# Graph-attention block on one core: value parts side by side in the attention product, head halves added on GpSimd

## The chip, the cores and the metric

The kernel runs on one core of one Trainium2 chip. The metric is device time in microseconds (us) of one execution, the median of several executions of the same program. Lower is better.

## What is computed

The reference chains two layers over 384 nodes with 1,024 features: a dense graph attention with 16 heads of width 64 (with a mask made of 6,144 edges), a linear attention and a quantised feed-forward block, then a second layer with a graph convolution of four hops, another linear attention and a mixture of eight experts. The change touches the 16-head attention, in float32 throughout:

```python
q2, k2, v2 = (each (N, H*D)).reshape(N, H, D).transpose(1, 0, 2)      # N = 384, H = 16, D = 64
scores = einsum('hnd,hmd->hnm', q2, k2) * 0.125 + mask[None]
attn = softmax(scores, axis=-1)
out = einsum('hnm,hmd->hnd', attn, v2).transpose(1, 0, 2).reshape(N, 1024)
return out @ wo.T + bo
```

## The kernel before, in words

Every engine has its own instruction stream, and all streams walk the same list of steps (`STEPS`, built by `schedule()`), each taking from a step what is its part. Nothing is reordered at run time: an engine that waits holds everything behind it in its stream.

Products in float32 precision are made of three passes of a faster format (fp32r): an operand is split into a high part (ScalarE: `hi_part`, a rounding copy) and a low part (VectorE: `lo_part`, the difference), and TensorE adds high x high, high x low and low x high. Weights come in 140 units of 128x1024: SyncE loads `raw`, ScalarE makes `w_hi` (L955), VectorE makes `w_lo` (L1263), three units ahead of TensorE (`AHEAD`), in a ring of four (`RING`).

The attention stage lies from about 218 to 357 us. For a head h the steps are `scores` (TensorE, L2014: two matmuls for each of three tiles of 128 rows; VectorE, L1580: moves each tile out of its bank, adds the mask and takes the row maximum; then L1585 makes `nmax` from the three maxima), `exps` (ScalarE, L1099), `normalise` (VectorE, L1596 and L1598), `probs` (TensorE transposes, L1829; ScalarE and VectorE make the two parts of `probT`) and `attend`: the product of probabilities and values. Two heads later the next scores are under way, and units of the next projections fill TensorE between: `k2` and `q2` up to head 11, the first five units of the output projection `wo` from head 12 on. A `k2` unit ends in `kcat` (ScalarE L946, VectorE L1472, and GpSimd copies it by two DMAs), a `q2` unit in `qcat`. Both use bank 0, so that a `q2` unit starts when VectorE has emptied the `k2` unit before it. `scores` reuses its banks when VectorE has moved the scores of the head before out of them.

In `attend` of head h the values are loaded as 128 columns, those of the even and of the odd head of a pair, so each product yields 128 rows, of which 64 are the head's own. High and low part of v2 are separate planes, and it takes nine matmuls. ScalarE and VectorE split the head's 64 rows into `oT`.

After the last head come `ffn_mean`, then the rest of `wo`: unit 5 ends the first half of the columns (c = 0), units 6 to 11 are the second half (c = 1), the last four of them row tile by row tile (L2069). ScalarE has between them `w_open` and `w_cast`, two long casts of feed-forward weights. VectorE moves the first half out by `wo_out(0, t)` (L1348, statistics behind it, L1278 and L1355), for three tiles, between the splits of later units; the feed-forward block starts on VectorE with `wo_out(1, 0)` in the step `in_stats`, when tile 0 of the second half is complete.

`wo_out` adds the product to `base1`, an array in SBUF that holds x and two bias rows. GpSimd makes it: SyncE loads x, then GpSimd issues three accumulating DMAs of the row `bo`, waits for them to land, and issues three of the row `mix_bo` (L812). Its code stands at the step of the last head:

```python
if s[0] == "attend" and s[1] == H0 - 1:
    pool.wait_ge(x_landed, 16)
    for t in range(NT):
        add_row("bo", t, base1).then_inc(bo_added, 16)
    pool.wait_ge(bo_added, 16 * NT)
    for t in range(NT):
        add_row("mix_bo", t, base1).then_inc(base1_ready, 16)
```

and the first line of `wo_out` is `dve.wait_ge(base1_ready, 16 * NT)`. Before the change GpSimd has no part in any other `attend` step; in that stage its stream holds only the copies of `kcat` and table work for the graph.

Of the kernel before, what the change touches and what calls it, by code (L numbers as in the profile page):

```python
# [5 lines left out]
F32 = mybir.dt.float32  # L6
# [9 lines left out]
P = 128  # L16
# [64 lines left out]
def schedule():  # L81
# [76 lines left out]
    run("wo", 5, 6)  # L158
    steps.append(("w_open",))
    run("wo", 6, 7)  # L160
# [132 lines left out]
def plan_banks():  # L293
# [12 lines left out]
    for s in STEPS:  # L306
        kind = s[0]
        if kind == "unit":
            _, u, name, i = s
            if name in FEATURE_MAJOR:  # L310
                if name in ("v1", "mk"):
                    product(f"{name}.{i}", i % 3 + 3 * (name == "mk"), u)
                elif name in ("q2", "k2"):
                    product(f"{name}.{i}", {("k2", 0): 1, ("k2", 1): 1, ("q2", 0): 4, ("q2", 2): 1}.get((name, i), 0), u)
                else:
                    product(f"{name}.{i}", i % 6 if name == "e1" else single % 6, u)
                    single += 1
            else:
                per = NODE_MAJOR[name][1]
                if i % per == 0:  # L320
                    for t in range(NT):

                        b = {("wo", 0): (0, 6, 1), ("e2", 0): (4, 5, 0), ("e2", 8): (1, 2, 3)}.get((name, i), tuple(range(
                            3 * (group % 2), 3 * (group % 2) + 3)))[t]
                        product(f"{name}.{i // per}.{t}", b, UNIT_OF[(name, i + per - 1)] if t == NT - 1 else None)
                    group += 1
# [86 lines left out]
def gps_kernel(nc, weights, x_in, edges, rows, cols, tiny, w1_in, w2_in, gate_in, eb2_in, out):  # L413
    with ExitStack() as ctx:
# [48 lines left out]
        v2 = at("v2", [P, 2, NT, D], F32R, R2)  # L463
# [4 lines left out]
        prob = at("prob", [P, 2, NT, N], F32, AT + 12)  # L468
        probT = at("probT", [P, 2, NT, N], F32R, AT + 21)
# [141 lines left out]
        s_max, s_exp, p_ready = sem("s_max"), sem("s_exp"), sem("p_ready")  # L611
# [14 lines left out]
        h_scaled = sem("h_scaled")  # L626
        out_ready, out_stored = sem("out_ready"), sem("out_stored")
# [52 lines left out]
        def row(name, a=0, b=None):  # L680
            return row_sb[:, row_slot(name)[0], a:sum(q - p for _, p, q in LOADS[name][1]) if b is None else b]

# [92 lines left out]
        def _(pool):  # L775
# [65 lines left out]
            for s in STEPS:  # L841
# [54 lines left out]
                if s[0] == "degree":  # L896
                    wait_emptied(pool, "degree")
                    pool.tensor_tensor(dis[:, 1], dis[:, 0], minus_half[:, 0:NT], ALU.pow).then_inc(dis_ready, 1)
                if s[0] == "attend" and s[1] == H0 - 1:

                    pool.wait_ge(x_landed, 16)
# [37 lines left out]
        def _(act):  # L939
# [58 lines left out]
            for s in EVAC_STEPS:  # L998
# [24 lines left out]
                if kind == "unit":  # L1023
# [23 lines left out]
                    if name in NODE_MAJOR and i % NODE_MAJOR[name][1] == NODE_MAJOR[name][1] - 1:  # L1047
                        c = i // NODE_MAJOR[name][1]
                        for t in range(NT):
                            pr = f"{name}.{c}.{t}"  # L1050
                            sl = slice(c * HALF, (c + 1) * HALF)
                            if name == "v2":
                                wait_emptied(act, pr)
                                hi_part(v2[:, 0, t, sl], v2f[:, t, sl])
# [39 lines left out]
                if kind == "exps":  # L1094
                    h = s[1]
                    act.wait_ge(s_max, h + 1)
                    for t in range(NT):

                        act.activation(prob[:, h % 2, t], prob[:, h % 2, t], ACT.Exp, scale=0.125,  # L1099
# [9 lines left out]
                if kind == "attend":  # L1109
# [4 lines left out]
                    hi_part(TT["o"][hs, 0, h // 2], out_of(f"attend.{h}")[hs, 0:N], f"attend.{h}")  # L1114
# [118 lines left out]
        def _(dve):  # L1233
# [170 lines left out]
            for s in EVAC_STEPS:  # L1404
# [50 lines left out]
                if kind == "unit":  # L1455
# [33 lines left out]
                    if name in NODE_MAJOR and i % NODE_MAJOR[name][1] == NODE_MAJOR[name][1] - 1:  # L1489
                        c = i // NODE_MAJOR[name][1]  # L1490
                        sl = slice(c * HALF, (c + 1) * HALF)
                        if name in ("v2", "v"):
# [7 lines left out]
                            for t in range(NT):  # L1500
                                wait_emptied(dve, f"{name}.{c}.{t}")
                                if name == "v2":
                                    low, high, src = v2[:, 1, t, sl], v2[:, 0, t, sl], v2f[:, t, sl]
# [63 lines left out]
                if kind == "scores":  # L1567
# [5 lines left out]
                    if h >= 1:  # L1573
                        dve.wait_ge(s_max, h)
# [25 lines left out]
                if kind == "attend":  # L1600
                    h = s[1]
                    hs = slice(64 * (h % 2), 64 * (h % 2) + 64)
                    lo_part(TT["o"][hs, 1, h // 2], out_of(f"attend.{h}")[hs, 0:N], TT["o"][hs, 0, h // 2], f"attend.{h}")
# [205 lines left out]
        def _(pe):  # L1809
# [35 lines left out]
            for s in STEPS:  # L1845
# [31 lines left out]
                if kind in ("unit", "part", "first_k"):  # L1877
# [44 lines left out]
                    else:  # L1922
# [7 lines left out]
                        for kk in [n % per for n in here]:  # L1930
# [6 lines left out]
                            elif name == "wo":  # L1937
# [3 lines left out]
                                if c == 0 and kk >= 2:  # L1941
                                    wait_emptied(pe, f"attend.{4 * kk - 5 - 2 * (kk == per - 1)}")
# [74 lines left out]
                if kind == "probs":  # L2017
                    h = s[1]
                    pe.wait_ge(p_ready, NT * (h + 1))
                    for m in range(NT):  # L2020
                        transposes(f"pT.{h}.{m}", [prob[:, h % 2, t, m * P:(m + 1) * P] for t in range(NT)])
                if kind == "attend":
# [5 lines left out]
                    js = slice(h // 2 * P, (h // 2 + 1) * P)  # L2028
# [57 lines left out]
                if kind == "in_T":  # L2086
                    t = s[1]
                    pr = f"xqT.{t}"
                    pe.wait_ge(in_quant, t + 1)
                    wait_bank(pe, pr)  # L2090
# [167 lines left out]
```

## Time and profile before

| | us |
|---|---|
| median of three runs | 756.64 |
| lowest and highest | 756.59, 757.14 |
| span of the profiled execution | 755.6 |
| TensorE busy in the span | 733.0 |
| VectorE busy | 547.4 |
| ScalarE busy | 391.2 |
| GpSimd busy | 193.3 |

The span runs from the first to the last instruction of the profiled execution, whose own total time is not listed apart; the median of the runs is 1.0 us above the span. The span is therefore used for differences, and the median for the total. A busy TensorE means that matmuls follow one another without a gap. A 384-column matmul shows about 334 ns from start to end, but a new one starts about every 174 ns, so counts are multiplied by the distance of starts.

### The profile page before, as it was taken

The page shows a single profiled execution, that of the slowest core. Times are in us where ns is not written, and L with a number is a line of the kernel's source. Part 1 is how long each engine was busy: PE and PEld are TensorE (multiplying, and loading weights), DVE is VectorE, ACT ScalarE, POOL GpSimd, SP SyncE. Part 2 cuts the span into 40 slices and gives each one's busy share as a digit, 9 for nine tenths or more (in the row PEclk, how much of TensorE's full clock was granted, in tenths as well). Part 3 has the DMA queues.
Part 4 walks back from the last instruction along what each step waited for, and adds up shares of the span by engine and source line. Part 5 has one row for each costly group of instructions (what it writes and reads, how often), then busy time and mean ns, then how long its engine had stood idle before and what let it go on. Part 6 is the DMA issues. An engine that isn't in the chain of part 4 may idle for free. (4 is left out here: it accounts for less than half of the span.)

```text
span 755.6 us, 10696 instructions
## 1 busy us (share of the span) xinstructions
PE 733.0 (97%) x3884; PEld 655.2 (87%) x3884; DVE 547.4 (72%) x1071; ACT 391.2 (52%) x802; POOL 193.3 (26%) x194
## 2 busy tenths in 40 slices
PE   5999999999999999999988999999999989999998
PEld 4999888999999999988755888888888889998886
DVE  6898885654569999876878687899966776674331
ACT  5533334644748767666665464854753342553220
POOL 5358888864205520021032110000020020000000
PEclk9999999999999999999999999999999999999999
DMA  7876555436434442499453582332352363244331
GB/s 253 304 208 170 115 137 140 112 85 224 142 105 130 101 109 77 164 286 267 136 137 112 152 227 88 134 122 74 112 125 84 119 131 137 96 142 151 126 126 42
DMA packets 38532, 107.71 MB, mean 143 GB/s; under 512 B 12424, under 2 KB 12600, under 8 KB 38096
## 3 DMA queue, kind: packets, MB, share of 16 engines
q1 hardware_dynamic: 25360, 89.90, 35.4%
q0 software_dynamic: 12912, 15.00, 12.5%
q10 hardware_dynamic: 208, 2.12, 0.8%
q8 instruction: 31, 0.51, 0.3%
q14 instruction: 21, 0.17, 0.1%
HBM read 96.31 MB, written 2.83 MB: 131 GB/s over the span
## 5 line engine op out<-in xcount | busy, mean ns | idle before, releaser
L1263 DVE TENSOR_TENSOR w_lo<-raw,w_hi 128x1024 fp32r<-128x1024 f32 x140 | 170.0, 1222 | 71.1 <-ACT w_hi L955 70.7
L955 ACT ACTIVATE w_hi<-raw 128x1024 fp32r<-128x1024 f32 x140 | 147.5, 1057 | 102.3 <-PE bank L1970 81.1
L1918 PE MATMUL bank<-xn1T,w_hi 128*128 128x384 f32 x416 | 106.1, 335 | 0.0
L1970 PE MATMUL bank<-w_hi,xn3T 128*128 128x512 f32 x288 | 92.6, 394 | 0.0
L816 POOL DMA_INDIRECT count_table<-total,place x48 | 82.9, 1727 | 26.5 <-issue 14.3
L1918 PEld LDWEIGHTS bank<-xn1T,w_hi 128*128 128x128 f32 x416 | 74.9, 188 | 0.1
L1918 PE MATMUL bank<-xn1T,w_lo 128*128 128x384 f32 x208 | 69.5, 334 | 0.0
L1970 PEld LDWEIGHTS bank<-w_hi,xn3T 128*128 128x128 f32 x288 | 54.1, 188 | 11.0
L816 POOL DMA_INDIRECT mask_table<-value,place x48 | 54.1, 1126 | 31.0 <-issue 13.1
L1918 PE MATMUL bank<-xn4T,w_hi 128*128 128x384 f32 x240 | 61.1, 335 | 0.0
L1970 PE MATMUL bank<-w_lo,xn3T 128*128 128x512 f32 x144 | 56.0, 389 | 0.0
L1918 PEld LDWEIGHTS bank<-xn4T,w_hi 128*128 128x128 f32 x240 | 43.2, 188 | 0.0
L1918 PE MATMUL bank<-xn4T,w_lo 128*128 128x384 f32 x120 | 40.2, 335 | 0.0
L1918 PEld LDWEIGHTS bank<-xn1T,w_lo 128*128 128x128 f32 x208 | 39.0, 188 | 0.0
L1099 ACT ACTIVATE prob<-prob,nmax 128x384 f32<-128x384 f32 x48 | 29.1, 609 | 10.9 <-DVE nmax L1585 10.7
L922 POOL DMA_DIRECT2D x_sb<-g x3 | 2.6, 1200 | 120.1 <-DVE g L1718 120.1
L890 POOL DMA_DIRECT2D kcat<-kcat x16 | 8.7, 546 | 96.1 <-DVE kcat L1472 95.2
L1918 PE MATMUL bank<-q1T,w_hi 128*128 128x384 f32 x128 | 33.1, 339 | 0.1
L1918 PE MATMUL bank<-k1T,w_hi 128*128 128x384 f32 x128 | 32.5, 335 | 0.0
L1970 PEld LDWEIGHTS bank<-w_lo,xn3T 128*128 128x128 f32 x144 | 27.1, 188 | 5.3
L1970 PE MATMUL bank<-w_hi,yT 128*128 128x512 f32 x96 | 31.0, 394 | 0.0
L1970 PE MATMUL bank<-w_hi,hT_a 128*128 128x512 f32 x96 | 30.6, 389 | 0.0
(353 smaller groups left out, 1682.7 us busy)
## 6 DMA issues: line engine op xcount, KB each, us to landing
raw<-weights SPq DMA_DIRECT2D x140, 512.0 KB, 3.6
row_sb<-rows SPq DMA_DIRECT2D x6, 512.0 KB, 6.0
kcat<-kcat POOLq DMA_DIRECT2D x16, 192.0 KB, 2.9
base<-rows POOLq DMA_DIRECT2D x6, 512.0 KB, 13.0
w1r<-w_in ACTq DMA_DIRECT2D x1, 2048.0 KB, 8.8
w2r<-w_in SPq DMA_DIRECT2D x1, 2048.0 KB, 10.3
x_sb<-x_in SPq DMA_DIRECT2D x3, 512.0 KB, 5.0
row_sb<-rows SPq DMA_DIRECT2D x6, 256.0 KB, 5.1
```

Of the source, the lines that this page charges most:

```text
L816: return pool.indirect_dma_start(tab[:, :], bass.IndirectOffsetOnAxis(ap=place[:, n:n + 1].bitcast(U32), axis=0), src, None, **how)
L890: pool.dma_start(f(kcat[other, r]), f(kcat[own, r])).then_inc(k_twice, 16)
L922: pool.dma_start(x_sb[:, t, HID:D], g[:, t], accum_op=ALU.add).then_inc(base3_ready, 16)
L955: act.activation(w_hi[:, u % RING], raw[:, u % RAW], ACT.Copy).then_inc(hi_split, 1)
L1099: act.activation(prob[:, h % 2, t], prob[:, h % 2, t], ACT.Exp, scale=0.125, bias=nmax[:, h % 2, t:t + 1], accum_out=rsum[:, h % 2, t:t + ...
L1263: dve.tensor_tensor(w_lo[:, u % RING], raw[:, u % RAW], f(w_hi[:, u % RING]), ALU.subtract).then_inc(unit_split, 1)
L1918: last = pe.matmul(out_of(pr)[:, 0:N], w[pa][:, slot, k * P:(k + 1) * P], TT[src][:, pb, k], start=(k == 0 and m == 0), stop=(k == KD - 1 ...
L1970: last = pe.matmul(out_of(pr)[:], tile[:, pa, k, ts], w[pb][:, at_, j * HALF:(j + 1) * HALF], start=(kk == 0 and j == 0 and m == 0 and nam ...
```

## The change

The parts of v2 lie side by side for each head: 64 columns of the high part, 64 of the low part. One matmul with the high part of `probT` then gives high x high in output rows 0 to 63 and the correction in rows 64 to 127, and `attend` has six matmuls in place of nine (with the low part of `probT`, the rows 64 to 127 get low x low too). The two halves must be added: ScalarE copies the lower 64 rows into `o_rest`, and after each odd head GpSimd adds `o_rest` (128x384, both heads of the pair) to the low part of `oT`. TensorE waits for that addition (`o_low`) where it reads `oT`, and for ScalarE's copy (`rest_kept`) before the bank is written again. The eviction of scores takes a scale of -0.125 and a minimum, so that it yields `nmax` and L1585 goes; ScalarE's exponentials wait for one tile at a time. In `wo`, unit 6 goes ahead of unit 5, with banks (4, 5, 3).

```diff
-    run("wo", 5, 6)
+    unit("wo", 6)
+    unit("wo", 5)
     steps.append(("w_open",))
-    run("wo", 6, 7)
     steps.append(("w_cast", 1))
...
-        v2 = at("v2", [P, 2, NT, D], F32R, R2)
+        v2 = at("v2", [P, NT, H0, 2 * DH], F32R, R2)
...
+        def v2_part(part, t, sl):
+            return v2[:, t, sl.start // DH:sl.stop // DH, part * DH:(part + 1) * DH]
...
         # GpSimd, ahead of the block for the step attend, H0 - 1
+                if s[0] == "attend" and s[1] % 2:
+                    j = s[1] // 2
+                    wait_emptied(pool, f"attend.{s[1]}")
+                    pool.wait_ge(rest_kept, s[1] + 1)
+                    pool.tensor_tensor(TT["o"][:, 1, j], f(TT["o"][:, 1, j]), o_rest[j % 2][:], ALU.add).then_inc(o_low, 1)
                 if s[0] == "attend" and s[1] == H0 - 1:
...
         # ScalarE
-                    act.wait_ge(s_max, h + 1)
+                        wait_emptied(act, f"scores.{h}.{t}")
-                        act.activation(prob[:, h % 2, t], prob[:, h % 2, t], ACT.Exp, scale=0.125,
+                        act.activation(prob[:, h % 2, t], prob[:, h % 2, t], ACT.Exp, scale=-1.0,
...
-                    hi_part(TT["o"][hs, 0, h // 2], out_of(f"attend.{h}")[hs, 0:N], f"attend.{h}")
+                    hi_part(TT["o"][hs, 0, h // 2], out_of(f"attend.{h}")[0:DH, 0:N], f"attend.{h}")
+                    if h >= 4:
+                        act.wait_ge(o_low, h // 2 - 1)
+                    act.activation(o_rest[h // 2 % 2][hs], out_of(f"attend.{h}")[DH:2 * DH, 0:N], ACT.Copy).then_inc(rest_kept, 1)
...
         # VectorE
-                        emptied(dve.tensor_tensor_reduce(out=prob[:, b, t], in0=out_of(pr)[:, 0:N], in1=mask[:, t], scale=1.0,
-                                                         scalar=-3.0e38, op0=ALU.add, op1=ALU.max,
-                                                         accum_out=top1[:, 0, t:t + 1]), pr)
-                    for t in range(NT):
-                        wait_emptied(dve, f"scores.{h}.{t}")
-                    dve.tensor_scalar(nmax[:, b], top1[:, 0], -0.125, None, ALU.mult).then_inc(s_max, 1)
+                        emptied(dve.tensor_tensor_reduce(out=prob[:, b, t], in0=out_of(pr)[:, 0:N], in1=mask[:, t], scale=-0.125,
+                                                         scalar=3.0e38, op0=ALU.add, op1=ALU.min,
+                                                         accum_out=nmax[:, b, t:t + 1]), pr)
...
         # TensorE
-                                    wait_emptied(pe, f"attend.{4 * kk - 5 - 2 * (kk == per - 1)}")
+                                    pe.wait_ge(o_low, 2 * kk - 2 - (kk == per - 1))
...
-                                wait_emptied(pe, f"attend.{H0 - 1}")
+                                pe.wait_ge(o_low, H0 // 2)
...
+                    if h:
+                        pe.wait_ge(rest_kept, h)
                     for m in range(NT):
                         pe.wait_ge(act_hi, hi_at[f"pT.{h}.{m}"])
-                        for part in (HI, LO):
-                            pe.matmul(out_of(pr)[:, 0:N], v2[:, part, m, js], probT[:, HI, m], start=(m == 0 and part == HI), stop=False)
+                        pe.matmul(out_of(pr)[:, 0:N], v2[:, m, h], probT[:, HI, m], start=(m == 0), stop=False)
                     for m in range(NT):
                         wait_emptied(pe, f"pT.{h}.{m}")
-                        last = pe.matmul(out_of(pr)[:, 0:N], v2[:, HI, m, js], probT[:, LO, m], start=False, stop=(m == NT - 1))
+                        last = pe.matmul(out_of(pr)[:, 0:N], v2[:, m, h], probT[:, LO, m], start=False, stop=(m == NT - 1))
```

## Rows read from the trace of the kernel before

**Rows 1.** The page, busy time of each engine

```profile
PE 733.0 (97%) x3884; PEld 655.2 (87%) x3884; DVE 547.4 (72%) x1071; ACT 391.2 (52%) x802; POOL 193.3 (26%) x194
```

**Rows 2.** Timeline of weight loads (PEld): start, length, engine, line, count, idle before

```profile
301.20 0.30 PEld L2014 LDWEIGHTS bank<-kcat,qcat 128*128 128x128 f32 x2 [0.18 <-DVE top L1580]
...
305.68 1.05 PEld L2033 LDWEIGHTS bank<-probT,v 128*128 128x128 f32 x6
306.72 0.53 PEld L2036 LDWEIGHTS bank<-probT,v 128*128 128x128 f32 x3
307.24 1.08 PEld L1829 LDWEIGHTS bank<-ident,prob 128*128 128x128 f32 x9
...
317.17 0.30 PEld L2014 LDWEIGHTS bank<-kcat,qcat 128*128 128x128 f32 x2 [0.18 <-DVE top L1580]
```

**Rows 3.** Timeline of VectorE over one pair of heads

```profile
290.75 1.26 DVE L1472 SCALAR_TENSOR_TENSOR kcat<-bank,bias,kcat 64x384 fp32r<-64x384 f32 x2 [0.86 <-ACT kcat L946]
...
293.48 0.09 DVE L1580 DVE_READ_ACCUMULATOR2_ANT top<- 128x1 f32 x1
293.70 0.17 DVE L1585 TENSOR_SCALAR nmax<-top 128x3 f32<-128x3 f32 x1
293.90 0.56 DVE L1254 TENSOR_TENSOR oT<-bank,oT 64x384 fp32r<-64x384 f32 x1
...
306.72 0.61 DVE L1472 SCALAR_TENSOR_TENSOR kcat<-bank,bias,kcat 64x384 fp32r<-64x384 f32 x1 [0.87 <-ACT kcat L946]
```

**Rows 4.** Groups of ScalarE in the attention stage, 215 to 375 us

```profile
L946 ACT ACTIVATE oT<-bank 64x384 fp32r<-64x384 f32 x16 | 7.8, 485 | 20.7 <-PE bank L2036 20.7
```

**Rows 5.** Busy time by stretch: TensorE, loads, VectorE, ScalarE, GpSimd, clock, DMA

```profile
350.00:355.00 5.00, 5.00 (x29) 4.30 (x28) 3.17 (x5) 4.57 (x6) 0.00 (x0) 1.00 1.06 236
360.00:365.00 5.00, 5.00 (x24) 4.14 (x23) 4.96 (x5) 4.81 (x3) 0.00 (x0) 1.00 0.04 13
```

**Rows 6.** Timeline of all engines after the last head's product

```profile
357.12 0.49 ACT L946 ACTIVATE oT<-bank 64x384 fp32r<-64x384 f32 x1 [0.51 <-PE bank L2036]
...
357.64 0.56 DVE L1254 TENSOR_TENSOR oT<-bank,oT 64x384 fp32r<-64x384 f32 x1 [3.37 <-ACT oT L946]
...
363.22 1.22 DVE L1263 TENSOR_TENSOR w_lo<-raw,w_hi 128x1024 fp32r<-128x1024 f32 x1
...
364.36 0.69 DVE L1348 CUSTOM_DVE_ANT_0 base<-bank,base 128x512 f32<-128x512 f32 x1
...
370.12 3.48 DVE L1263 TENSOR_TENSOR w_lo<-raw,w_hi 128x1024 fp32r<-128x1024 f32 x3
...
371.39 0.19 PEld L2069 LDWEIGHTS bank<-w_hi,oT 128*128 128x128 f32 x1 [0.88 <-DVE w_lo L1263]
...
375.92 0.69 DVE L1348 CUSTOM_DVE_ANT_0 base<-bank,base 128x512 f32<-128x512 f32 x1 [2.31 <-PE bank L2069]
```

**Rows 7.** Timeline of GpSimd, 320 to 380 us

```profile
326.36 2.73 POOL L812 DMA_DIRECT2D base<-rows  x3 [1.04 <-issue]
344.19 2.60 POOL L812 DMA_DIRECT2D base<-rows  x3 [15.09 <-DMA base<-rows]
377.69 0.19 POOL L868 TENSOR_SCALAR power_in<-mv 128x1 f32<-128x1 f32 x1 [30.91 <-DVE mv L1621]
```

**Rows 8.** DMA queues and issues, 310 to 400 us (issues: KB, us to landing)

```profile
q0 software_dynamic: 1425, 5.22, 29.0%
...
base<-base POOLq DMA_DIRECT2D x3, 512.0 KB, 4.7
```

**Rows 9.** DMA issues of GpSimd, 345.2 to 347 us

```profile
base<-rows POOLq DMA_DIRECT2D x2, 512.0 KB, 13.8
```

**Rows 10.** DMA issues of GpSimd, 434 to 438 us

```profile
x_sb<-rows POOLq DMA_DIRECT2D x3, 512.0 KB, 9.4
```

**Rows 11.** Groups of GpSimd over the whole span

```profile
L831 POOL TENSOR_SCALAR_AFFINE_SELECT later<-later 128x896 f32<-128x896 f32 x1 | 1.8, 1804 | 0.1
```

**Rows 12.** Timeline of the first weight loads of the kernel

```profile
9.41 1.36 PEld L1858 LDWEIGHTS bank<-ident,xn_nat 128*128 128x128 f32 x7 [6.08 <-ACT xn_nat L995]
```

More of the change, by code:

```diff
@@ L321, in plan_banks @@
                     for t in range(NT):
-                        b = {("wo", 0): (0, 6, 1), ("e2", 0): (4, 5, 0), ("e2", 8): (1, 2, 3)}.get((name, i), tuple(range(
+                        b = {("wo", 0): (0, 6, 1), ("wo", 6): (4, 5, 3), ("e2", 0): (4, 5, 0), ("e2", 8): (1, 2, 3)}.get((name, i), tuple(range(
                             3 * (group % 2), 3 * (group % 2) + 3)))[t]
@@ L468, in gps_kernel @@
         prob = at("prob", [P, 2, NT, N], F32, AT + 12)
+        o_rest = [at(f"o_rest{n}", [P, N], F32, ROWS_AT + 6 + 4 * n) for n in range(2)]
         probT = at("probT", [P, 2, NT, N], F32R, AT + 21)
@@ L610, in gps_kernel @@
         mctx_f, mctx_ready = sem("mctx_f"), sem("mctx_ready")
-        s_max, s_exp, p_ready = sem("s_max"), sem("s_exp"), sem("p_ready")
+        s_exp, p_ready = sem("s_exp"), sem("p_ready")
         k_half, k_twice = sem("k_half"), sem("k_twice")
@@ L626, in gps_kernel @@
         h_scaled = sem("h_scaled")
+        rest_kept, o_low = sem("rest_kept"), sem("o_low")
         out_ready, out_stored = sem("out_ready"), sem("out_stored")
@@ L1053, in _ @@
                                 wait_emptied(act, pr)
-                                hi_part(v2[:, 0, t, sl], v2f[:, t, sl])
+                                hi_part(v2_part(0, t, sl), heads(v2f[:, t, sl]))
                             if name == "v":
@@ L1502, in _ @@
                                 if name == "v2":
-                                    low, high, src = v2[:, 1, t, sl], v2[:, 0, t, sl], v2f[:, t, sl]
+                                    low, high, src = v2_part(1, t, sl), v2_part(0, t, sl), heads(v2f[:, t, sl])
                                 else:
@@ L1572, in _ @@
                         wait_full(dve, "mixo.3")
-                    if h >= 1:
-                        dve.wait_ge(s_max, h)
                     if h >= 2:
@@ L1602, in _ @@
                     hs = slice(64 * (h % 2), 64 * (h % 2) + 64)
-                    lo_part(TT["o"][hs, 1, h // 2], out_of(f"attend.{h}")[hs, 0:N], TT["o"][hs, 0, h // 2], f"attend.{h}")
+                    lo_part(TT["o"][hs, 1, h // 2], out_of(f"attend.{h}")[0:DH, 0:N], TT["o"][hs, 0, h // 2], f"attend.{h}")
                 if kind == "ffn_mean":
@@ L2019, in _ @@
                     pe.wait_ge(p_ready, NT * (h + 1))
+                    if h == 1:
+                        pe.wait_ge(rest_kept, 1)
                     for m in range(NT):
@@ L2027, in _ @@
                     wait_bank(pe, pr)
-                    js = slice(h // 2 * P, (h // 2 + 1) * P)
+                    if h:
+                        pe.wait_ge(rest_kept, h)
                     for m in range(NT):
                         pe.wait_ge(act_hi, hi_at[f"pT.{h}.{m}"])
-                        for part in (HI, LO):
-                            pe.matmul(out_of(pr)[:, 0:N], v2[:, part, m, js], probT[:, HI, m], start=(m == 0 and part == HI), stop=False)
+                        pe.matmul(out_of(pr)[:, 0:N], v2[:, m, h], probT[:, HI, m], start=(m == 0), stop=False)
                     for m in range(NT):
                         wait_emptied(pe, f"pT.{h}.{m}")
-                        last = pe.matmul(out_of(pr)[:, 0:N], v2[:, HI, m, js], probT[:, LO, m], start=False, stop=(m == NT - 1))
+                        last = pe.matmul(out_of(pr)[:, 0:N], v2[:, m, h], probT[:, LO, m], start=False, stop=(m == NT - 1))
                     full(last, pr)
@@ L2089, in _ @@
                     pe.wait_ge(in_quant, t + 1)
+                    pe.wait_ge(rest_kept, H0)
                     wait_bank(pe, pr)
```

## The prediction

> **What bounds the kernel now.** I read the busy times first: TensorE is busy for 733.0 of the 755.6 us of the span, so matmuls that go should be worth their time, unless something else paces the stage they are in [rows 1]. So I looked at the stage. In the timeline of weight loads, the nine matmuls of one head's attention product start at 305.68 and the transposes behind them at 307.24: 1.56 us for nine, 0.173 us each [rows 2]. The same rows show TensorE stopping inside the next scores, 0.18 us at 301.20 and again at 317.17, each time until VectorE has moved a tile of scores out. These two points are one pair of heads apart, 15.97 us.
>
> VectorE's timeline tells who paces that pair. It starts on `kcat` at 290.75 and again at 306.72, also 15.97 us, and its only idle time in between is the 0.87 us ahead of `kcat` [rows 3]. The ring is: `kcat`, a string of VectorE's work up to the second head's scores (301.07 or so), TensorE's last scores matmuls, the `k2` unit (301.49 to 305.68), ScalarE's high part, `kcat`. The attention product is not in it: it lies ahead of the scores, where TensorE then waits [rows 2, 3].
>
> From head 12 on the filler is `wo`, VectorE has room, and TensorE is busy for all of 350 to 355 us [rows 5]. After the last product (ScalarE takes it up at 357.12) I followed VectorE: `oT` ends at 358.20, a split of weights, then `wo_out(0, 0)` at 364.36, the three of them until 370.12, then the splits for which TensorE stands from 370.5 to 371.39, and at 375.92 the first tile of the second half starts the feed-forward chain [rows 6]. Last I read GpSimd, whose stream the change lengthens: the three `bo` additions go out at 326.36, the three `mix_bo` additions at 344.19 after a wait of 15.09 us for the first ones, and the last of them lands about 359 to 360 [rows 7, 9]. That is 4 to 5 us before `wo_out(0, 0)` asks for them. This small reserve decides the change.
>
> **Part 1, nine matmuls to six.** 3 x 0.173 = 0.52 us a head, 8.3 us for 16 heads. Where VectorE paces, it is not collected: the stop inside the scores grows by it. Also, a `q2` unit needs bank 0 emptied by `kcat`, which ends at about 307.98, while TensorE now reaches it at 308.3 [rows 2, 3]; it could come only 0.3 us sooner. I count the 0.52 us for heads 12 to 15 alone: 2.1 us.
>
> **Part 2, the eviction yields the bias.** From the end of the accumulator read (293.57) to `oT` (293.90) lie 0.33 us, which go [rows 3]. Of the two in a pair one lies in the ring: four pairs give 1.3 us, heads 1 to 3 (VectorE is as full there) about 1.0. The minimum form of the eviction has no row; I take the maximum's time. The other bound is twice its 0.55 us, 48 x 0.5 = 24 us more; nothing reported speaks for it, since width and operands are the same.
>
> So the last product ends 2.1 + 1.3 + 1.0 = 4.4 us sooner. Bounds: 1 us, if nearly all is lost to new contention, and 8.3 us, if VectorE follows TensorE everywhere.
>
> **Part 3, ScalarE's copy and GpSimd's addition.** The copy is like the high part beside it, 0.485 us [rows 4], 16 of them, and ScalarE waited 20.7 us in all ahead of the high parts: hidden, and the exponentials start sooner in exchange. The 128x384 addition has no row. Bounds: GpSimd's 128x896 select at 2.0 ns an element gives 0.77 us [rows 11], two inputs instead of one at most double it. I take 0.8 us. For heads 1 to 13 it is hidden behind ten matmul-filled microseconds until someone reads `oT`. If its SBUF traffic slows VectorE beside it, at most as long as it lasts, 7 x 1.5 us are at stake, and with it the 4.4 us.
>
> **Part 4, what stands behind the addition on GpSimd.** The stream is in order, and the new wait for head 15's product stands ahead of the six additions of bias rows. Now they were issued at 326.36; after the change they can't go before head 15 is split. I count on the clock of the old trace, from the end of the last product at 357.1. `oT` low ends at 358.2 (ScalarE's copy meanwhile), the addition at 359.1 [rows 6, 11].
>
> Price of a batch of three: queue 0 carried 5.22 MB in 29.0% of 90 us, 26.1 us of all 16 engines, 5.0 us per MB, so 2.6 us for 512 KB; one such DMA alone takes 4.7 us, so some 2.0 us are latency [rows 8]. A batch needs 2.0 + 3 x 2.6 = 9.9 us if nothing else runs. In 360 to 365 us the DMA engines are at 0.04 [rows 5], and only some weight units come in, so I take 10.5 us. Lower bound 9.9, upper 12.2 (a batch of three issued at 434.66 beside weight loads, median 9.4 to landing from each issue, the last issued later) [rows 10]. The two batches run one after the other because of the wait on `bo_added`: 359.1 + 0.2 + 21 = 380.3.
>
> `wo_out(0, 0)` now starts there and not at 364.36. Behind it on VectorE: 5.76 us until the third tile is done (386.1), then the split of unit 10, 1.2 us (387.3), which TensorE needs after units 8 and 9 of the first tile; unit 10 takes 1.4 us, unit 11 waits for its own split (388.5) and ends at 390.0. The feed-forward chain begins at 390.1 and not at 375.92: 14.2 us later. TensorE stands idle from about 372 to 387. Everything behind it hangs on this chain and moves along.
>
> **Part 5, unit 6 ahead of unit 5.** It covers the way through the copy and GpSimd, 2 us, by 4.1 us of matmuls: no wait for `o_low`. But ScalarE then makes unit 9's high part before `w_open`, waiting for unit 6 to end. By itself this moves the splits by about 2 us and takes away the 0.88 us stop at 371.39 [rows 6]; inside the 14.2 us it is hidden. Free.
>
> **Part 6, the clock.** At the start of the kernel, after 6.08 us idle, seven transposes take 1.36 us, 0.20 us apart; in the attention stage nine take 1.08, 0.12 apart [rows 2, 12]. If TensorE comes back from 15 idle microseconds at that rate, the 12 matmuls of units 10 and 11 (2.8 us) take up to 2.8 us more. I take 2.0; bounds 0 and 2.8. The Trainium skill says so much (TensorE: Matmul & The Clock Gate, "Part 1: The HAM clock gate"): the throttled state is the default, at half rate, and activity releases it. The rows above agree with a slow start; no row of before shows a long idle gap in mid-kernel.
>
> **Sum.** -4.4 + 14.2 + 2.0 = +11.8 us. Taken off the span and carried to the median (1.0 us above it): 756.6 + 11.8 = 768.4.
>
> **Rivals.**
> 1. All of the 8.3 us are collected (VectorE's waits turn out to be TensorE's doing): 764.5. Against it: 0.87 us of idle in 15.97 [rows 3]. Chance 0.12.
> 2. The additions land at the rate of plain copies and the delay is small. A batch must take 5.6 us and not 9.9 for gain and loss to cancel: 357.1 + 2.2 + 11.2 = 370.5, chain at 380.3, +4.4 - 4.4 = 0, 756.6. Against it the 4.7 us of a single one [rows 8]. The Trainium skill has just this price (DMA: Bandwidth & Descriptors, "Anatomy of one DMA — SWDGE (gpsimd) path"): about 2.0 us plus bytes at 436 GB/s, 3.2 us for 512 KB, 5.6 for three. The trace's 4.7 disagrees: these DMAs accumulate. Chance 0.06.
> 3. Faster: VectorE doesn't need the bias rows late, because GpSimd isn't held (the additions are out and landed by the time of 364.36). Place: GpSimd's stream at head 15; it decides when both batches land within 13 us of the last product's end. It would give 756.6 - 4.4 = 752.2. Against it the order of the stream. Chance 0.06.
> 4. The DMA engines are as crowded as in 326 to 360, where the first batch held GpSimd for 17.8 us and the second landed after some 15 [rows 7, 9]: 33 in place of 21 us, 780. Against it the share of 0.04. Chance 0.06.
> 5. VectorE gets slower: port contention with GpSimd's additions eats the 4.4 us (773), or the minimum form is slower (up to 792). Chance 0.08.
>
> **How the numbers follow.** My forecast has 0.62. Its own range is 764 to 773: batches of 9.9 to 12.2 each, clock 0 to 2.8, gain 3 to 6. The range for 8 in 10 reaches over rival 1 and the milder part of 5, with the bounds of gain, batches and clock taken partly together: 761 to 776. A change of 0.2% (1.5 us) is about what a measurement of this kernel can tell from none. Faster: rival 3 and a bit of 2, 0.08. Same: most of rival 2, 0.04. Slower: 0.88.
>
> **What the profile after would show.** Six loads in `attend` and about 96 matmuls in all; pairs of heads 15.6 us apart and not 14.9, with the stop inside the scores grown; the last product about 352.7; the first `base<-rows` issue near 355 and not 326; VectorE idle for about 15 us before the first L1348, released by a DMA; TensorE idle as long inside L2069; the granted clock down after it. It is wrong if L1348 starts without such a wait, if the pairs come 1 us closer together, or if a batch lands in 6 us.

## The result, and the profile after

The changed kernel takes 774.64 us (median of 4, 773.22 to 775.16), the kernel before beside it 756.89 (756.59 to 757.43): a ratio of 1.0234 [1.0221, 1.0247], 17.8 us slower. The profiled execution took 773.22 us, its span is 771.4. TensorE has 50 matmul records fewer than in [rows 1] (by the code it is 48), and is busy 5.0 us less, while the span is 15.8 us longer. First the page of the kernel after: busy times, then TensorE and its granted clock in 40 slices of 19.3 us.

```profile
PE 728.0 (94%) x3834; PEld 648.4 (84%) x3836; DVE 546.2 (71%) x1055; ACT 400.0 (52%) x818; POOL 207.5 (27%) x202
...
PE   5999999999999999999197999999999999999998
...
PEclk9999999999999999999689999999999999999999
```

The hole is in slice 20, 366 to 386 us. GpSimd's timeline shows what leads to it, and VectorE's what ends it (start, length, engine, line, output<-input, count, idle before and its releaser):

```profile
354.84 1.01 POOL L910 TENSOR_TENSOR oT<-oT,o_rest 128x384 fp32r<-128x384 f32 x1 [12.12 <-DVE oT L1269]
356.40 4.92 POOL L818 DMA_DIRECT2D base<-rows  x3 [0.55 <-issue]
369.66 2.59 POOL L818 DMA_DIRECT2D base<-rows  x3 [8.33 <-DMA base<-rows]
393.53 0.19 POOL L874 TENSOR_SCALAR power_in<-mv 128x1 f32<-128x1 f32 x1 [21.28 <-DVE mv L1631]
```

```profile
354.21 0.55 DVE L1269 TENSOR_TENSOR oT<-bank,oT 64x384 fp32r<-64x384 f32 x1 [2.88 <-ACT oT L958]
...
355.18 2.82 DVE L1624 TENSOR_SCALAR w2r<-w2r,w_s 128x4096 f32<-128x4096 f32 x1
...
360.25 2.35 DVE L1278 TENSOR_TENSOR w_lo<-raw,w_hi 128x1024 fp32r<-128x1024 f32 x2
380.03 0.69 DVE L1363 CUSTOM_DVE_ANT_0 base<-bank,base 128x512 f32<-128x512 f32 x1 [17.43 <-DMA base<-rows]
...
385.80 2.35 DVE L1278 TENSOR_TENSOR w_lo<-raw,w_hi 128x1024 fp32r<-128x1024 f32 x2
391.76 0.69 DVE L1363 CUSTOM_DVE_ANT_0 base<-bank,base 128x512 f32<-128x512 f32 x1 [3.61 <-PE bank L2081]
```

The bias rows are issued at 356.40 and not at 326.36 [rows 7], each batch of three waits for the one before, and `wo_out(0, 0)` (now L1363) starts at 380.03, released by a DMA; before it started at 364.36 and waited for nothing [rows 6]. The feed-forward chain begins at 391.76 and not at 375.92. TensorE stands in between, in the timeline of its weight loads:

```profile
353.72 0.30 PEld L2054 LDWEIGHTS bank<-w_s,ones 128*128 128x128 f32 x2 [1.08 <-ACT w2q L1134]
...
387.07 0.29 PEld L2081 LDWEIGHTS bank<-w_hi,oT 128*128 128x128 f32 x1 [18.26 <-DVE w_lo L1278]
```

Its granted clock, by stretches (columns: busy time of TensorE, loads, VectorE, ScalarE, GpSimd, then clock, DMA share, GB/s): it falls to 0.50, which is 1.2 GHz, in a stretch in which TensorE does nothing, is still there at 389 to 390 us, and is back at full rate, 2.4 GHz, at 391. TensorE's matmuls begin again at 387.07.

```profile
372.00:373.00 1.00, 0.00 (x0) 0.00 (x0) 0.00 (x0) 0.52 (x2) 0.25 (x1) 1.00 1.11 221
373.00:374.00 1.00, 0.00 (x0) 0.00 (x0) 0.00 (x0) 0.00 (x0) 0.00 (x0) 0.64 1.08 213
374.00:375.00 1.00, 0.00 (x0) 0.00 (x0) 0.00 (x0) 0.00 (x0) 0.00 (x0) 0.50 1.06 193
...
389.00:390.00 1.00, 1.00 (x4) 0.81 (x3) 0.00 (x0) 0.00 (x0) 0.00 (x0) 0.50 1.02 393
...
391.00:392.00 1.00, 1.00 (x6) 0.83 (x5) 0.24 (x1) 0.00 (x0) 0.00 (x0) 1.00 0.95 352
```

**What balances against what.** The attention stage is not entered at the same time in every profiled execution, although nothing ahead of it differs but the places into which the parts of v2 are written (its first scores are at 218.18 before, at 216.89 after). Kernels with the change cover the whole spread themselves: 216.42 in e6, 218.10 in e1, 218.18 in e7. So I compare lengths inside it. From the first scores to the end of the last product: 138.9 us before (357.08 - 218.18), 136.1 after (352.97 - 216.89), a gain of 2.8. From there to the feed-forward chain, which VectorE starts with `wo_out(1, 0)`: 18.84 us before, 38.79 after, a loss of 19.95. The balance, +17.1, is what the medians show (+17.8); the earlier entry makes it +15.8 in the two spans.

### The profile page after: what moved, and what is told of

It is laid out like the page before. It is cut to its first block and busy times, and to the rows that moved or that the text cites. A ratio compares the mean times of both kernels' runs of the same rounds, so it can differ in the third digit from the quotient of the medians.

```text
span 771.4 us, 10597 instructions
## 1 busy us (share of the span) xinstructions
PE 728.0 (94%) x3834; PEld 648.4 (84%) x3836; DVE 546.2 (71%) x1055; ACT 400.0 (52%) x818; POOL 207.5 (27%) x202
## 3 DMA queue, kind: packets, MB, share of 16 engines
HBM read 96.31 MB, written 2.83 MB: 129 GB/s over the span
## 5 line engine op out<-in xcount | busy, mean ns | idle before, releaser
L822 POOL DMA_INDIRECT count_table<-total,place x48 | 87.0, 1812 | 25.5 <-issue 14.0
L2081 PE MATMUL bank<-w_hi,oT 128*128 128x512 f32 x48 | 17.1, 425 | 17.8 <-DVE w_lo L1278 17.8
```

The lines of the kernel that those rows point to most:

```text
L822: return pool.indirect_dma_start(tab[:, :], bass.IndirectOffsetOnAxis(ap=place[:, n:n + 1].bitcast(U32), axis=0), src, None, **how)
L2081: last = pe.matmul(out_of(pr)[:], tile[:, pa, k, ts], w[pb][:, u % RING, j * HALF:(j + 1) * HALF], start=(kk == 0 and j == 0 and m == 0), ...
```

## Experiments

Twelve kernels ran; the kernel before ran beside each (medians 757.2, 756.9 and 756.6 us in the three sets). The edits are against the kernel after, where nothing else is said.

**e1: the bias rows go out early, all else as changed.** In GpSimd's stream the six additions leave their place behind head 15.

```diff
-if s[0] == "attend" and s[1] == H0 - 1:    # 3 x bo, wait, 3 x mix_bo
+if s[:4] == ("unit", UNIT_OF[("k2", 7)], "k2", 7):
+    pool.wait_ge(x_landed, 16)              # 3 x bo
+if s[0] == "attend" and s[1] == 13:
+    pool.wait_ge(bo_added, 16 * NT)         # 3 x mix_bo
```

> The changed kernel, with GpSimd's additions of the bias rows taken out from behind the last head's addition: bo at the last k2 unit, mix_bo at head 13. Theory (the order of GpSimd's stream makes the whole loss): no wait of VectorE for a DMA before its first eviction of wo, the feed-forward chain starts about 3.5 us sooner than in the kernel before (372.4 and not 375.9), 753.4 us. Rival (the six-matmul form or GpSimd's work on its own costs time too): 758 to 770. Rival (all 8.3 us of the matmuls come in once the delay is gone): 749.

Measured: 754.74 us (754.0 to 755.56), ratio 0.9963 [0.995, 0.9977]. GpSimd and VectorE in its timeline:

```profile
324.69 2.71 POOL L818 DMA_DIRECT2D base<-rows  x3 [1.04 <-issue]
326.42 2.08 POOL L910 TENSOR_TENSOR oT<-oT,o_rest 128x384 fp32r<-128x384 f32 x1
342.98 1.02 POOL L910 TENSOR_TENSOR oT<-oT,o_rest 128x384 fp32r<-128x384 f32 x1 [14.48 <-DVE oT L1269]
343.95 2.76 POOL L818 DMA_DIRECT2D base<-rows  x3
```

```profile
363.79 0.68 DVE L1363 CUSTOM_DVE_ANT_0 base<-bank,base 128x512 f32<-128x512 f32 x1
...
374.00 0.69 DVE L1363 CUSTOM_DVE_ANT_0 base<-bank,base 128x512 f32<-128x512 f32 x1 [2.10 <-PE bank L2081]
```

The wait is gone and with it the whole loss: 19.9 us between two kernels that compute the same and differ in where six transfers stand in one queue. What is left of the change is worth 2.5 us.

**e2: the kernel before, its bias rows held until head 15's low part.** The loss without the change.

```diff
 # in the kernel before
+wait_emptied(pool, f"attend.{H0 - 1}")
 pool.wait_ge(x_landed, 16)
```

> The kernel before, with nothing changed but that the additions of the bias rows wait on GpSimd for the last head's low part. Theory: issues start at 358.3 and not at 326.4, the two batches take 13.2 and 10.4 us as in the changed kernel, TensorE comes back at 1.2 GHz for about 1.8 us more, the chain starts 17 to 18 us later: 774.5 us. Rival (the loss comes from the new product or the copies): within 3 us of 756.9.

Measured: 778.09 us (777.21 to 779.33), ratio 1.0281 [1.0265, 1.0297], 3.6 more than expected. In its timelines:

```profile
358.55 4.72 POOL L812 DMA_DIRECT2D base<-rows  x3 [34.25 <-issue]
372.39 2.59 POOL L812 DMA_DIRECT2D base<-rows  x3 [9.12 <-DMA base<-rows]
```

```profile
382.67 0.69 DVE L1349 CUSTOM_DVE_ANT_0 base<-bank,base 128x512 f32<-128x512 f32 x1 [19.25 <-DMA base<-rows]
```

The mechanism alone makes a slow kernel of the old one. Batch 1 took 13.84 us and batch 2 10.28. From `wo_out(0, 0)` to the chain it is 13.06 us, against 11.73 in the kernel after. In the old order of the units three splits of weights stand behind `wo_out` and not two, and the first one is unit 9's: TensorE comes back as soon as in the kernel after (1.26 us behind the third `wo_out`, at 389.70), but has 18 matmuls to do and not 12, 6.03 us and not 4.69. So with the bias rows late the swapped units, which I had called free, seem to save these 1.3 us; no run swapped them alone in that state.

**e3: `bo` early, `mix_bo` late.** Half of the serial wait.

```diff
+if s[:4] == ("unit", UNIT_OF[("k2", 7)], "k2", 7): ...   # 3 x bo, as in e1
 if s[0] == "attend" and s[1] == H0 - 1: ...              # 3 x mix_bo only
```

> The changed kernel with bo added early and only the mix_bo batch behind the last head. Theory (the two batches are simply in series): one batch of 10.4 to 13.3 us less, VectorE starts evicting wo at 367 to 370, the chain at 379 to 381.5, so 760 to 762.5 us. Rival (the loss is a fixed cost of coming late, such as GpSimd's issue beside VectorE): above 768.

Measured: 763.93 us (763.34 to 764.41), ratio 1.0087 [1.0072, 1.0103]. GpSimd's issue of the one batch, and VectorE's release by it:

```profile
356.18 5.53 POOL L818 DMA_DIRECT2D base<-rows  x3
```

```profile
370.32 0.69 DVE L1363 CUSTOM_DVE_ANT_0 base<-bank,base 128x512 f32<-128x512 f32 x1 [7.34 <-DMA base<-rows]
```

That is 14.14 us for one batch. It is the first batch behind head 15, not the second, that is longer than the 10.5 I had assumed.

**e5 and e6: which of the two gains is real.** e5 is the kernel before with the eviction of the scores that yields the bias (-0.125 and minimum, exponentials released tile by tile); e6 is e1 with the old eviction (maximum, then `nmax` in an instruction of its own), so six matmuls alone.

```diff
 # e5, in the kernel before (e6: the reverse, in e1)
-dve.tensor_scalar(nmax[:, b], top1[:, 0], -0.125, None, ALU.mult).then_inc(s_max, 1)
-... scale=1.0,    scalar=-3.0e38, op0=ALU.add, op1=ALU.max, accum_out=top1[:, 0, t:t + 1]
+... scale=-0.125, scalar=3.0e38,  op0=ALU.add, op1=ALU.min, accum_out=nmax[:, b, t:t + 1]
```

> The kernel before with the new eviction of scores alone (scale -0.125, minimum, no nmax instruction, exponentials released tile by tile), nine matmuls kept. Theory (VectorE paces pairs of heads): 0.33 us for heads 1 to 3 each and for each of four pairs, 2.3 us: 754.6 us, pairs 15.6 us apart. Rival (TensorE paces): no change, 756.9. Rival (the minimum form is slower): above 757.

> The changed kernel with the bias rows added early and the old eviction (maximum, then nmax). Theory: six matmuls alone are worth 0.52 us only in heads 12 to 15, 2.1 us less what the tail takes back: 755 to 755.8 us; the difference to the version with the new eviction is 1.5 to 2.3 us. Rival (the matmuls are worth their 8.3 us in all heads): 749 to 751.

Measured: e5 755.5 us, ratio 0.998 [0.9971, 0.9989]; e6 755.68, ratio 0.9988 [0.998, 0.9997]. So by the ratios 1.5 us for the eviction (0.8 to 2.2 by its interval) and 0.9 for the nine-to-six matmuls (0.2 to 1.5), 2.4 together, and e1 with both has 2.5 to 2.8. The 8.3 us of matmuls are not collected, as the prediction had it against its first rival.

**e4: e1 without the swap.** Units 5 and 6 in the old order, in the old banks.

```diff
-unit("wo", 6)
-unit("wo", 5)
+run("wo", 5, 6)
 steps.append(("w_open",))
+run("wo", 6, 7)
```

> The changed kernel with the bias rows added early (bo at the last k2 unit, mix_bo at head 13) and unit 5 of wo ahead of unit 6 again, with the old banks. Theory (the swap covers a wait that the first halves of unit 5 nearly cover by themselves, and trades one late split for another): within 1 us of the version with the swap. Rival (the swap is worth its 2 us of covered latency): 2 us slower than that version. Rival (the swap's late split of unit 9 costs more): 1 us faster or better.

Measured: 754.42 us (753.75 to 755.24, 8 runs), ratio 0.9969 [0.9959, 0.998]. It can't be told from e1. With the bias rows early the swap neither gains nor costs anything that these runs can show.

**e7: the additions of the bias rows wait for VectorE's passes over `w2r` too.** GpSimd's issue of the first three takes 4.92 us, and only 2.73 in [rows 7]; beside it run VectorE's two passes of 128x4096. I held the long issue to be the reason for the long batch.

```diff
+pool.wait_ge(w_unit, 2)
 pool.wait_ge(x_landed, 16)
```

> The changed kernel, where the additions of the bias rows wait also for the end of VectorE's two 4,096-element passes over w2 (360.3). Theory (GpSimd's issues take 4.92 us in place of 2.7 because VectorE's fast passes keep it from writing descriptors): the three issues take 2.6 to 2.8 us, the first batch about 10.4 in place of 13.3, the chain starts only 1 to 1.5 us later for issues that start 4 us later: 776 us. Rival (a batch takes 13.3 us at this place whatever runs beside): 4 us later, 778.7.

Measured: 780.59 us, ratio 1.0317 [1.0304, 1.033].

```profile
362.41 2.70 POOL L818 DMA_DIRECT2D base<-rows  x3 [5.86 <-issue]
375.65 2.59 POOL L818 DMA_DIRECT2D base<-rows  x3 [10.54 <-DMA base<-rows]
```

The issue is short again (2.70), and the batch takes 13.24 us all the same. The theory fell as I had put it: the long issue is not what makes the batch long here. The kernel is 5.9 us slower than the one after; counted from the first scores its issue starts 4.7 us later, batch 2 takes 0.3 us more, and from `wo_out(0, 0)` to the chain it is 0.9 us more (the granted clock is still 0.50 at 398 to 399 us; TensorE's matmuls begin again at 393.35).

**e9: the loads of two weight units are held until the bias rows are in.**

```diff
+if (name, i) == ("wo", 11):
+    sp.wait_ge(base1_ready, 16 * NT)
```

> The changed kernel, in which SyncE holds the loads of the weight units wo 11 and g1 0 until the bias rows are added. Theory (the first batch of additions takes 13.3 us where the second takes 10.4 because those two loads share the DMA engines with it): first batch 10.4 to 11.3 us, the second unchanged, 2 to 2.9 us faster than the changed kernel, 772 to 772.7 us. Rival (GpSimd's slow issue, 4.92 us beside VectorE's passes, sets the length): the first batch stays above 12.8 us, no gain.

Measured: 773.16 us, ratio 1.0219 [1.0205, 1.0233]. Batch 1 took 12.29 us (356.40 to 368.69), 1.0 less, batch 2 10.20. That is neither the theory's 10.4 to 11.3 nor the rival's 12.8 and more. Three views of the DMA during batch 1 answer e7 and e9 together: after, 356.40 to 369.66; e7, 362.41 to 375.65; e9, 356.40 to 368.69. The digits are the busy share of the 16 engines in 40 slices of the stretch; q0 carries the bias rows, q1 the weights. After:

```profile
DMA  0000000948999999999999999699995999989999
...
q0 software_dynamic: 432, 1.57, 67.7%
q1 hardware_dynamic: 220, 0.84, 17.5%
```

e7:

```profile
DMA  0093999696699998999998997999999999997000
...
q0 software_dynamic: 432, 1.57, 64.7%
q1 hardware_dynamic: 288, 1.05, 25.9%
```

e9:

```profile
DMA  0000000491799999999999999999989997100000
...
q0 software_dynamic: 432, 1.57, 69.6%
```

The three rows cost the 16 engines nearly the same in each: 9.0, 8.6 and 8.6 us (share by length of stretch). What differs is what else the engines carry: 2.3 us of weights in the kernel after, 3.4 us in e7, none in e9. The bias rows start late in all three. In the kernel after and in e9 nothing moves until the eighth slice, 2.3 and 2.2 us behind the issue. In e7 packets go from the third slice on, but these are weights; until 365.00, 2.6 us behind the issue, queue 0 has sent nothing:

```profile
q1 hardware_dynamic: 109, 0.45, 70.8%
```

So the short issue of e7 brought no earlier start of the bias rows; until they start, only weights are on the engines. Each of the two runs took one thing away, and neither batch became as short as a second batch, which takes 10.2 to 10.9 us over these kernels. In e9, with no weights, the first batch is still 2.1 us longer than its own second. The 1.0 us of e9 is itself the difference of two single traces: in e8 (next), whose extra matmuls begin only at 368.2, batch 1 took 13.85 us, 0.6 more than in the kernel after. A kernel with a short issue and no weights beside it was not run, so how the rest divides stays open.

**e8: TensorE kept busy in the gap.** 95 extra matmuls of 384 columns into a free bank, whose result nobody reads, after unit 9 of the first tile.

```diff
+if t == 0 and (name, n) == ("wo", 2):
+    wait_emptied(pe, "pT.15.1")
+    for _ in range(95):
+        pe.matmul(bank[2][:, 0:N], w_hi[:, UNIT_OF[("wo", 9)] % RING, 0:P], TT["o"][:, HI, 0], ...)
```

> The changed kernel with 95 matmuls of 384 columns into an unused bank where TensorE waits for unit 10 of wo (extra work, its result is not read). Theory (the clock falls to 1.2 GHz because TensorE stands idle): granted clock 1.00 throughout, the 12 matmuls of units 10 and 11 take 2.8 us and not 4.6, 1.8 us faster than the changed kernel, 772.8 us. Rival (the slow restart has another cause, such as late splits): no difference.

Measured: 772.88 us (772.02 to 773.51), ratio 1.021 [1.0197, 1.0223], 1.8 us under the kernel after. Over the kernel after's four executions the mean granted clock is 0.986 to 0.989; of e8's five it is 1.0 in three (772.34, 772.88, 772.02) and 0.997 and 0.998 in two (773.41, 773.51). The profiled one is of the two, and its stretches show why:

```profile
386.00:387.00 1.00, 0.00 (x0) 0.00 (x0) 1.00 (x2) 0.00 (x0) 0.00 (x0) 1.00 0.00 0
...
388.00:389.00 1.00, 1.00 (x6) 0.84 (x5) 0.69 (x1) 0.00 (x0) 0.00 (x0) 0.99 0.39 66
389.00:390.00 1.00, 1.00 (x4) 0.72 (x3) 0.00 (x0) 0.00 (x0) 0.00 (x0) 0.50 0.91 340
```

The clock stayed up through the filler, and fell for 3 us after the 2.5 us in which TensorE still waited for unit 10's split. Besides, its two batches took 13.85 and 10.91 us, 1.1 more than in the kernel after. So this trace alone shows no gain over the one after; the median of the three executions at full clock does (772.34 against 774.64, 2.3 us).

**e11: ScalarE's pass over `w2r` two heads earlier** (in e4). After head 15's product `oT` high has to wait for this 3.63 us pass, and TensorE stops 1.09 us for its result.

```diff
-if h == H0 - 1:
+if h == H0 - 3:
     steps.append(("ffn_abs", 1))
```

> The version without the swap and with the bias rows early, and ScalarE's pass of absolute values over w2 (3.8 us) two heads earlier, at head 13. Theory (TensorE stops 0.75 us after the last product because the mean of |w2| waits for this pass, which the shorter product has left uncovered): the stop goes, oT of head 15 starts 0.7 us sooner, 0.5 to 0.8 us faster than that version (754.4): 753.7. Rival (the pass at head 13 holds up ScalarE's splits of oT and probT there): no gain or slower.

Measured: 754.73 us (753.57 to 756.19), ratio 0.9977 [0.9967, 0.9987]. The stop is gone, and the pass (338.39 to 342.1) now delays head 13's `oT`: first scores to last product takes 136.4 us, 135.5 in e4. Nothing is won.

**e12 and e13: is it VectorE alone that paces the pairs?** VectorE normalises one of three tiles, in e4 (e12) and in the kernel before (e13); both kernels leave out the normalisation of the other two tiles.

```diff
-for t in range(NT):
-    dve.tensor_scalar(prob[:, h % 2, t], prob[:, h % 2, t], rsum[:, h % 2, t:t + 1], ...).then_inc(p_ready, 1)
+dve.tensor_scalar(prob[:, h % 2, 0], prob[:, h % 2, 0], rsum[:, h % 2, 0:1], ...).then_inc(p_ready, NT)
```

> The version without the swap and with the bias rows early, where VectorE normalises one of the three tiles of probabilities only (the other two stay unnormalised), 0.72 us less of its work a head. Theory (VectorE paces the pairs of heads, TensorE has 14.5 us of work in each): pairs fall from 15.6 to about 14.6 us, 4 to 5.5 us faster than that version: 749.5 us. Rival (something else, such as ScalarE or the banks, paces once TensorE is lighter): pairs stay above 15.3.

> The kernel before, with the same cut: VectorE normalises one of three tiles of probabilities only. Theory (TensorE has 15.6 us of work in a pair with nine matmuls a head, VectorE's ring now 14.5): pairs fall from 15.97 to 15.6 only, 1.5 to 3 us faster than the kernel before: 754.6 us. With the same cut the six-matmul version then wins 5 us and not 2.5. Rival (VectorE alone sets both): both kernels gain the same.

Measured: e12 752.73 us, ratio 0.9947 [0.9933, 0.996], pairs of 15.38 to 15.40 (a fifth one 16.40); e13 754.61, ratio 0.9975 [0.9966, 0.9985], pairs of 15.65 to 15.76 (and 16.66). e13's own time came as expected, e12's not: 1.7 us gained and not 5. The cut is worth about the same in both kernels (1.7 and 1.9 us by the ratios), and e12 stands 1.9 us under e13, not 5: making VectorE lighter did not set the matmuls' gain free. VectorE's timeline of e12:

```profile
292.47 0.42 DVE L1607 TENSOR_SCALAR prob<-prob,rsum 128x384 f32<-128x384 f32 x1
293.14 1.23 DVE L1278 TENSOR_TENSOR w_lo<-raw,w_hi 128x1024 fp32r<-128x1024 f32 x1 [0.25 <-ACT w_hi L967]
...
299.55 0.18 DVE L1606 RECIPROCAL rsum<-rsum 128x3 f32<-128x3 f32 x1 [0.49 <-ACT prob L1111]
...
302.74 1.26 DVE L1487 SCALAR_TENSOR_TENSOR kcat<-bank,bias,kcat 64x384 fp32r<-64x384 f32 x2 [1.01 <-ACT kcat L958]
```

Two things are seen. The normalisation lies in the ring once a pair, not twice: from `kcat` to the second head's last scores (the part that holds one) it is 10.09 us in the kernel after and 9.83 in e12, while the rest of the pair (last scores to next `kcat`) is 5.54 and 5.55. And of the 0.66 us that the one cut saves, 0.4 is lost at once, 0.25 of it in the wait of `w_lo` for ScalarE's `w_hi`, which stands behind three exponentials, two high parts, and the new copy of 0.48 us. I read from this that VectorE paces, with ScalarE right behind it; no run made ScalarE lighter.

## Why the prediction was right, and where it was off

It said slower by 11.8 us, 768.4, range 761 to 776. It was slower by 17.8, 774.64: the sign and the mechanism right, inside the range near its end, and outside the likeliest case's own range of 764 to 773. By its steps:

**Part 1, matmuls.** Right that the pairs don't collect them. The pair that took 15.97 us takes 15.63 (`kcat` 288.48 to 304.11), and its loads show where the 1.04 us of six matmuls went:

```profile
288.48 1.07 PEld L1839 LDWEIGHTS bank<-ident,prob 128*128 128x128 f32 x9
289.86 0.30 PEld L1928 LDWEIGHTS bank<-q1T,w_hi 128*128 128x128 f32 x2 [0.30 <-issue]
...
297.73 0.71 PEld L2024 LDWEIGHTS bank<-kcat,qcat 128*128 128x128 f32 x4 [0.61 <-issue]
298.63 0.30 PEld L2024 LDWEIGHTS bank<-kcat,qcat 128*128 128x128 f32 x2 [0.18 <-DVE nmax L1593]
```

TensorE stops 1.09 us a pair: 0.61 and 0.18 in the scores, and 0.30 ahead of the `q2` unit, where it comes too early for bank 0 (VectorE empties it by `kcat`, until 289.74). Before it stopped 0.38, of which I had named 0.18 (the other, 0.20, is no row of the text). 1.04 less 0.71 is the 0.33 that the pair gained. For heads 12 to 15 I had counted all 2.1 us; they gave 1.2 (from the last `kcat` to the last product 33.84 before, 32.63 after). The stops there grew from 1.05 to 2.39 us in all, and TensorE had come 0.5 us further when that `kcat` began (its product of head 11 ended 0.5 us ahead of it). Of the four stops of after, VectorE is named as the releaser of 0.27 and 0.42 us; the other two, 0.87 and 0.83, name none. So TensorE alone does not pace this stretch either.

**Part 2, the eviction.** The minimum form takes 0.55 us like the maximum. From the end of the accumulator read (291.30) to `oT` (291.33) nothing is left of the 0.33 us. Four pairs gave 1.1 us (15.94, 15.97, 15.97, 16.52 became 15.79, 15.65, 15.63, 16.23) for 1.3, the first heads 0.5 for 1.0. Together the last product comes 2.8 us sooner for the 4.4 of the sum: 1.6 too much.

**Part 3, copy and addition.** The copy takes 0.49 us. The addition takes 1.01 us where I took 0.8, 1.58 and 1.60 in two of the earlier heads, and up to 2.08 right behind GpSimd's own DMA issues (e1). VectorE's work in the pairs was not slower for it; its first pass over `w2r`, whose start runs beside head 15's addition, was: 2.82 or 2.83 us in the ten kernels with that addition, 2.35 in the four without it (before, e2, e5, e13).

**Part 4, the stream behind the addition.** This is the cause, and e1 and e2 show it from both sides: moving six transfers takes all of the loss out of the new kernel and puts more than it into the old one. Its size, term by term. From the end of the last product to the issue: 3.43 us, 2.2 in the sum, because ScalarE's pass over `w2r` (until 353.66) holds `oT` high (0.7), the addition is longer (0.2), and GpSimd lets 0.55 us pass between addition and issue where the sum had 0.2. Batch 1: 13.26 us, 10.5 in the sum, and over my upper bound of 12.2. Batch 2: 10.37, 10.5 in the sum. From `wo_out(0, 0)` to the chain: 11.73, 11.8 in the sum with the clock. So the term that was mis-sized is the first batch, 2.8 of the 3.8 us that this part was short. I had read the DMA share of 0.04 at 360 to 365 us [rows 5] and taken it for the whole batch, of which it covers half. The second half is not free, in the trace of before already: its queue 1 carries most of a load of weights at 366 to 370 us (packets, MB, share of the 16 engines), and in the kernel after nearly two. Before, then after:

```profile
q1 hardware_dynamic: 125, 0.45, 30.3%
```

```profile
q1 hardware_dynamic: 249, 0.95, 63.1%
```

About 1.0 us went when two of the loads were held (e9), and that figure carries the 0.6 us by which the same batch differs between two traces. The rest is not accounted for. By ever narrower windows on queue 0, the bias rows' first packets leave 2.2 to 2.7 us after the issue in the first batches (3.0 in e3), and 1.6 to 1.9 in the second ones. VectorE's passes over `w2r` go with the long issue: it took 4.72 us in e2, 4.92 in three kernels and 5.53 in e3 beside them, and 2.70 in e7 behind them. But e7 shows that a short issue does not shorten the batch when weights are beside it, and no run had neither.

Rival 2 fell too: the shortest batch of this study took 10.20 us with nothing beside it (e9's second), 8.5 of them with all 16 engines busy for 1.57 MB. The price of the Trainium skill for this path (DMA: Bandwidth & Descriptors, "Anatomy of one DMA — SWDGE (gpsimd) path"), from which 5.6 us were worked out as an estimate, disagrees with the traces for these accumulating transfers, which took 10.20 us and more.

**Part 5, the swap.** Free is right for the good kernel (e4 against e1); in the slow one it is worth about 1.3 us, if e2 is read rightly.

**Part 6, the clock.** 2.0 in the sum. The same 12 matmuls of units 10 and 11 take 4.69 us in the kernel after, from their first load to the chain (387.07 to 391.76), and 3.18 in e1 (370.82 to 374.00), where the clock is full:

```profile
370.82 0.19 PEld L2081 LDWEIGHTS bank<-w_hi,oT 128*128 128x128 f32 x1 [0.77 <-DVE w_lo L1278]
```

So the clock costs 1.5 us in this trace; in e7 it is 2.4 (5.63 us for the same matmuls), and e8's medians give 1.8 to 2.3. The term was about right, 0.5 too high in this trace; the way from `wo_out(0, 0)` to the chain without the clock was 0.4 too low (10.2 us and not 9.8), so that the two nearly cancel, which is luck. The rule that the prediction cites from the Trainium skill (TensorE: Matmul & The Clock Gate, "Part 1: The HAM clock gate") agrees: the granted clock fell to half in idle time and rose again after matmuls.

**The sum by what was measured.** -2.8 for the last product, and +19.95 behind it: 1.2 (later issue), 2.8 (batch 1), -0.1 (batch 2) and -0.1 (the rest) on top of the 16.2 that the prediction had, = 20.0. That is +17.1 for the +11.8 of the forecast; of the 5.3 us between them 1.6 are too much gain, and 3.7 or 3.8 too little loss.

**The rivals.** 1 fell with the pairs and e6. 3 (GpSimd not held) fell at the first row of its timeline, but its direction was right: e1 and e4 are what it describes, about 2.5 us faster and not 4.4. Its condition, both batches landed within 13 us of the last product's end, does not fit the sum beside it: `wo_out(0, 0)` stands 9.8 us ahead of the chain, so for no loss they have to land by 366.1, within 9 us. 4 was too high, 23.6 us for both batches and not 33. 5 fell in its price: contention is seen in one place, 0.5 us on the first pass over `w2r`, and the minimum form costs nothing.

## What to carry to other kernels

Before you put a wait into an in-order queue, list what stands behind it, and for each when its reader needs it: here 20 us hung on six transfers that had a reserve of 4 to 5 us and cost nothing to issue 30 us earlier. The change itself is good once they are moved: 754.4 to 754.7 us, 0.3% under the kernel before, and that is the version to keep. And read the DMA's share over the whole length of the transfer that you move, not over its beginning. Where an engine doesn't set the pace, a saving on it is idle time at the next meeting point; look for that point before counting the saving.

## What was not expected of the hardware

- GpSimd's issue of three accumulating transfers took 4.7 to 5.5 us while VectorE ran its 128x4096 passes (five kernels), 2.6 to 2.8 elsewhere. VectorE's pass was not longer for the issue (2.35 in e2, beside an issue of 4.72), but for GpSimd's addition (2.82).
- A 128x384 addition of GpSimd's takes 1.01 us alone, and 2.08 directly behind GpSimd's DMA issues (e1); the two spans overlap by a microsecond in the record.
- The same batch of three accumulating transfers, on the same instruction streams up to it, took 13.26 us in one trace and 13.85 in another (the kernel after, e8), and a batch with nothing else on the engines took 12.29 us as the first and 10.20 as the second (e9).
- In e8 2.5 us without matmuls, behind 17 us of filler, were followed by 3 us at half clock in the profiled execution, while three executions of the same kernel were granted the full clock throughout.
